# Cross attention beside its neighbours: one batch's chain in two groups, setup products in spare PSUM columns, even steps of a normalisation

## The reference

```
x = x + attention(ln1(x), ln1(x)) @ Wo1 + bo1        # 16 heads of 16, self
x = x + attention(ln2(x), ctx)   @ Wo2 + bo2         # the same, over 77 context rows ("cross")
h = ln3(x) @ Wff1 + bff1;  lin, g = split(h)
x = x + (lin * (g * sigmoid(1.702 g))) @ Wff2 + bff2 # inner width 1024
Q = x @ Wq.T + bq; K = ctx @ Wk.T + bk; V = ctx @ Wv.T + bv
x = rms_norm(softmax(Q K.T / 16) V @ Wfc.T + bfc + x) * w   # one head of 256
```

## Time and profile before

| | |
|---|---|
| median of 3 runs | 742.64 us (739.92 to 743.47) |
| the profiled execution | 749.67 us, its span 747.7 us |
| PE, DVE, ACT, POOL busy | 89%, 72%, 65%, 13% of the span |
| mean granted TensorE clock | 0.956 of full |
| chain of work that ended last, by engine | PE 64%, DVE 18%, ACT 10%, issue 5% |

### The profile page before, as it was taken

One profiled execution on the slowest core, in us unless ns is written; L12 is line 12 of the kernel. 1 busy time (PEld: TensorE's weight loads), 2 busy tenths in 40 slices (PEclk: granted clock), 3 DMA queues, 4 the chain that ended last, 5 costly groups with the idle time before them and its releaser, 6 DMA issues.

```text
span 747.7 us, 11140 instructions
## 1 busy us (share of the span) xinstructions
PE 667.3 (89%) x4072; PEld 320.0 (43%) x4072; DVE 536.1 (72%) x925; ACT 485.6 (65%) x845; POOL 93.8 (13%) x144
## 2 busy tenths in 40 slices
PE   3989799999999999999999888788798999999991
PEld 2644122222222222222224344235356878888881
DVE  6678989999999999999984538546743754343357
ACT  3543399999999999999998654447463233332374
POOL 2071800000000000000000201264101110000001
PEclk9999699999999999999999998779898999999996
DMA  9457350202020110100000020120000000000003
GB/s 301 182 169 253 95 196 1 72 1 71 1 71 2 43 30 1 29 2 29 1 2 1 31 91 23 46 70 31 3 1 1 0 1 1 1 1 1 1 0 113
DMA packets 35113, 36.87 MB, mean 49 GB/s; under 512 B 6132, under 2 KB 28276, under 8 KB 34804
## 3 DMA queue, kind: packets, MB, share of 16 engines
q1 hardware_dynamic: 33904, 35.87, 14.8%
q0 software_dynamic: 1024, 0.24, 0.3%
q10 hardware_dynamic: 132, 0.07, 0.0%
HBM read 23.09 MB, written 12.74 MB: 48 GB/s over the span
## 4 chain that ended last, share of the span: by engine, by line
PE 64%; DVE 18%; ACT 10%; issue 5%; DMA 1%; POOL 1%; SPq 0%; ACTq 0%; DVEq 0%; POOLq 0%
PE ps L934 15%; PE ps L922 10%; DVE mm L1557 7%; PE ps L718 6%; ACT probs L1317 6%; PE ps L1120 4%; PE ps L1121 4%; PE ps L1122 4%; PE ps L751 4%; PE ps L895 3%; PE ps L704 2%; PE ps L1037 2%; PE ps L726 2%; PE ps L1136 2%; DVE tok L1535 2%
## 5 line engine op out<-in xcount | busy, mean ns | idle before, releaser
L1317 ACT ACTIVATE probs<-ps,unfit 128x512 f32<-128x512 f32 x512 | 311.7, 691 | 28.6 <-PE ps L922 24.1
L1557 DVE TENSOR_REDUCE mm<-ps 128x2 f32<-128x1024 f32 x256 | 299.4, 1219 | 13.9 <-PE ps L751 9.8
L922 PE MATMUL ps<-stack 50*128 50x512 f16 x512 | 146.8, 388 | 7.2 <-ACT probs L1317 1.2
L934 PE MATMUL ps<-probs,v 128*32 128x512 f32 x1024 | 137.2, 608 | 2.7 <-ACT outT L1322 2.7
L751 PE MATMUL ps<-stack 48*128 48x512 f16 x512 | 108.5, 391 | 12.7 <-DVE mm L1557 6.6
L922 PEld LDWEIGHTS ps<-stack 50*128 50x128 f16 x512 | 36.9, 93 | 172.7 <-ACT probs L1317 164.7
L1417 ACT ACTIVATE early<-ps,cols 128x512 f32<-128x512 f32 x32 | 22.1, 690 | 91.8 <-PE ps L1122 91.8
L1813 DVE SCALAR_TENSOR_TENSOR hid<-ps,cols,early 128x512 f32<-128x512 f32 x32 | 24.0, 749 | 76.0 <-PE ps L1122 76.0
L612 POOL TENSOR_TENSOR x<-x,rows 128x512 f32<-128x512 f32 x24 | 31.9, 1343 | 164.0 <-DVE tok L1535 163.9
L1120 PE MATMUL ps<-x_hi,wff_hi 128*128 128x512 f32 x128 | 52.2, 408 | 0.0
L1372 ACT ACTIVATE probs<-ps,unfit 96x1024 f32<-96x1024 f32 x32 | 35.5, 1109 | 25.1 <-PE ps L1028 25.0
(11 more groups left out here) (168 smaller groups left out, 861.8 us busy)
## 6 DMA issues: line engine op xcount, KB each, us to landing
v_groups<-early SPq DMA_DIRECT2D x8, 512.0 KB, 3.1
stack<-q_parts SPq DMA_DIRECT2D x64, 64.0 KB, 2.0
v<-v_groups SPq DMA_DIRECT2D x8, 512.0 KB, 4.1
x<-in_x SPq DMA_DIRECT2D x4, 512.0 KB, 6.9
q_parts<-probs SPq DMA_DIRECT2D x8, 256.0 KB, 3.8
k_parts<-probs SPq DMA_DIRECT2D x8, 256.0 KB, 2.2
stack<-k_parts SPq DMA_DIRECT2D x16, 128.0 KB, 2.5
stack<-q_parts SPq DMA_DIRECT2D x64, 32.0 KB, 1.9
```

What stands on the lines that cost most here:

```text
L922: eng.matmul(ps[:, st_bank(n), :], stack[rows_of(tile, KROWS), SLOTS + slot, q, P * kc:P * kc + P], qs[rows_of(tile, KROWS), slot, half, q ...
L934: mm_ = eng.matmul(ps[32 * h:32 * h + 32, PV, :], v1[:, G % 2, kc, 32 * h:32 * h + 32], probs[:, k % 2, h, :], start=(kc == 0), stop=(kc = ...
L1317: eng.activation(probs[:, k % 2, HEADS[h], :], ps[:, st_bank(n), :], ACT.Exp, scale=unfit[:, 0:1]).then_inc(exp_done, 1)
L1557: eng.tensor_reduce(dst, ps[:, 2 * slot:2 * slot + 2, :], AX.X, ALU.max).then_inc(s_red, 1)
```

## The change

- Batch 1's chain(0,1) gets its nine pieces of the cross stage in groups 0 and 1, where they were spread over 0, 1 and 2. chain(1,0) gets all twelve of its pieces in groups 4 to 7; its last one, the turn of ln3's block 1, stood in the feed forward behind widen(0) before. `x_high(0)` and `x_low(0)` move one unit ahead.
- The first seven setup products are computed in columns 312 to 465 of banks 0 and 1, beside the 312 columns of the cross scores, just ahead of `scores_2` of tiles 10, 14, 15, 17, 19, 21 and 23, that is in (1,0), (2,0), (2,1), (2,3), (3,1), (3,3) and (4,1). DVE reads each after those scores and ahead of their maxima. The last two stand in columns 0 to 255 of these banks, after (7,0) and (7,2). Four waits of the chains and of `final_setup` go.
- `tick` goes out of `reduce_2`; each cross unit, each `add` and each `attended_2` now has tick(3).
- On SP, `load_max_2(2)` and `load_max_2(3)` stand later, behind loads of queries, and `load_q2(5)`'s first half stands behind the last store of queries.
- At the start PE turns block 0 ahead of `tops(0)`, and DVE takes `fit_scales(0)` after the statistics of block 1. POOL adds the third bias row only once eight `widen` steps are done.

```diff
-        PIECES = ((0, 1, 1, 0), (1, 1, 1, 2), (1, 1, 0, 0), (0, 0, 0, 0),
-                  (0, 0, 1, 1), (1, 1, 1, 2), (1, 1, 1, 1), (0, 0, 0, 0))
-        SETUPS = {(2, 2): 1, (2, 3): 2, (3, 1): 1, (7, 0): 1, (7, 1): 2, (7, 2): 1, (7, 3): 1}
-        SETUP_EARLY = 4
+        PIECES = ((2, 1, 1, 1), (1, 1, 1, 1), (0, 0, 0, 0), (0, 0, 0, 0),
+                  (0, 0, 1, 1), (2, 1, 2, 1), (1, 1, 0, 1), (0, 1, 0, 0))
+        SETUP_TILES = (10, 14, 15, 17, 19, 21, 23)
+        SETUPS = {(7, 0): 1, (7, 2): 1}
+        SPARE = HG * CTXE
+        def setup_col(k):
+            return SPARE if k < SETUP_1 + SETUP_2 - B else 0
...
@@ sync
             load_q2(3)
             load_max_2(1)
-            load_max_2(2)
             for u in range(half, half + NC):
                 store_parts(u)
             parts_stored(eng, half + NC)
-            for G in (4, 5):
-                eng.wait_ge(st_full, 64 * GROUPS + UNITS * (G - 3))
-                load_q2(G, (0,))
+            eng.wait_ge(st_full, 64 * GROUPS + UNITS)
+            load_q2(4, (0,))
+            load_max_2(2)
             for u in range(half + NC, len(PROJ)):
                 store_parts(u)
-            load_max_2(3)
+            eng.wait_ge(st_full, 64 * GROUPS + 2 * UNITS)
+            load_q2(5, (0,))
             parts_stored(eng, len(PROJ))
             load_q2(4, (1,))
             load_q2(5, (1,))
+            load_max_2(3)
@@ gpsimd, bias rows
+                if n == 2:
+                    eng.wait_ge(ff_full, FC)
@@ tensor
+            turn(LN1, 0)
             tops(0)
-            turn(LN1, 0)
@@ setup / final_setup
-                    bank = CHAIN + k % 2
+                    at = setup_col(k)
+                    out = ps[0:m, k % 2, at:at + n]
...
-                eng.wait_ge(rest_done, len(PROJ))
-                eng.wait_ge(su_done, SETUP_1 + SETUP_EARLY)
-                eng.wait_ge(y_added, TILES + KC)
-                turned(LN3, 0)
+                eng.wait_ge(su_done, SETUP_1 + NC)
...
+                eng.wait_ge(s2_red, KC // 2 * GROUPS)
@@ chain
-                if (n, b) == (1, 0):
-                    eng.wait_ge(su_done, SETUP_1 + SETUP_EARLY)
-                    if (ln, blk) == (LN3, 1):
-                        eng.wait_ge(su_done, SETUP_1 + SETUP_2)
@@ scores_2
                 if n >= 1:
                     eng.wait_ge(s2_red, n)
+                if n in SETUP_TILES:
+                    next(fillers)
@@ feed forward, on tensor, scalar and vector alike
+            eng.wait_ge(su_done, SETUP_1 + SETUP_2)      # tensor only
-            last_piece, after_cross = after_cross, chain(1, 1)
+            after_cross = chain(1, 1)
-                    advance(last_piece, 1)
@@ scalar, vector: x_high(0) after (7,0), was (7,1); x_low(0) after (7,1), was (7,2)
@@ vector
+                if blk == 1:
+                    fit_scales(0)
                 norm(0, blk)
-                if blk == 0:
-                    fit_scales(0)
@@ vector, chain after each add
-                    tick(4)
+                    tick(3)
@@ vector, reduce_2, attended_2, cross_unit
                 eng.wait_ge(s2_full, n + 1)
+                if n in SETUP_TILES:
+                    next(fillers)
...
-                tick(2)
...
                 attended(2 * GROUPS + 2 * G + half, MISC)
-                tick(2)
+                tick(3)
...
                     reduce_2(*divmod(ahead, UNITS))
+                tick(3)
                 advance(pieces, PIECES[G][d] // 2)
```

More of the change, by code:

```diff
@@ L301, in build @@
         AHEAD = 7
-        PIECES = ((0, 1, 1, 0), (1, 1, 1, 2), (1, 1, 0, 0), (0, 0, 0, 0),
-                  (0, 0, 1, 1), (1, 1, 1, 2), (1, 1, 1, 1), (0, 0, 0, 0))
-        SETUPS = {(2, 2): 1, (2, 3): 2, (3, 1): 1, (7, 0): 1, (7, 1): 2, (7, 2): 1, (7, 3): 1}
-        SETUP_EARLY = 4
+        PIECES = ((2, 1, 1, 1), (1, 1, 1, 1), (0, 0, 0, 0), (0, 0, 0, 0),
[3 more added lines that the diff above has]
+        SPARE = HG * CTXE
         FF_PIECES = (0, 0, 2, 2, 2, 2, 2, 2)
         assert sum(TAIL) == CHAIN_1 == AHEAD + sum(sum(PIECES[G]) for G in range(GPB))
-        assert sum(FF_PIECES) == CHAIN_2 == 1 + sum(sum(PIECES[G]) for G in range(GPB, GROUPS))
+        assert sum(FF_PIECES) == CHAIN_2 == sum(sum(PIECES[G]) for G in range(GPB, GROUPS))
         LINEAR, GATE, WIDE = 4, 5, (0, 1, 6, 7)
@@ L825, in setup @@
                 if k < SETUP_1:
-                    bank = 6 + k
+                    out = ps[0:m, 6 + k, 0:n]
                     eng.wait_ge(v_done, TILES - 1 + k)
                 else:
-                    bank = CHAIN + k % 2
+                    at = setup_col(k)
+                    out = ps[0:m, k % 2, at:at + n]
                     if k >= SETUP_1 + 2:
@@ L832, in setup @@
                 for i, (lhs, rhs) in enumerate(terms):
-                    mm_ = eng.matmul(ps[0:m, bank, 0:n], lhs, rhs, start=(i == 0), stop=(i == len(terms) - 1))
+                    mm_ = eng.matmul(out, lhs, rhs, start=(i == 0), stop=(i == len(terms) - 1))
                 mm_.then_inc(su_full, 1)
@@ L1073, in cross_unit @@
                 advance(pieces, PIECES[G][d] - PIECES[G][d] // 2)
+            fillers = final_setup()
             eng.wait_ge(mask_in, 16 * HT)
@@ L1098, in _ @@
             advance(after_self, 2)
-            fillers = final_setup()
             for G in range(GROUPS):
@@ L1398, in _ @@
                     cross_unit(G, d, after_self if G < GPB else after_cross)
-                    if (G, d) == (LAST, 1):
+                    if (G, d) == (LAST, 0):
                         x_high(0)
@@ L1420, in _ @@
                     hid_high(n - 1)
-                if n == 0:
-                    advance(last_piece, 1)
                 if n < FC:
@@ L1727, in read @@
                     eng.wait_ge(su_full, k[0])
-                    return ps[0:m, CHAIN + (k[0] - 1) % 2, 0:n]
+                    at = setup_col(k[0] - 1)
+                    return ps[0:m, (k[0] - 1) % 2, at:at + n]
                 for dst, c0 in ((kT, COL_BK), (vT, COL_BV)):
@@ L1799, in _ @@
                     advance(fillers, SETUPS.get((G, d), 0))
-                    if (G, d) == (LAST, 2):
+                    if (G, d) == (LAST, 1):
                         x_low(0)
```

## The result

Timed side by side on one chip, twenty executions each, the changed kernel took 743.30 us (median; 737.35 to 745.61) against 747.21 us (738.59 to 751.37): a ratio of 0.9947, 95% interval 0.9928 to 0.9966. It is faster by 0.5%, about 4 us, where 14 were forecast: 728.6 was predicted, and 743.3 lies outside of the range of 720 to 740. Of the 14.7 us between 728.6 and 743.3, 4.6 are not the change's: the forecast was counted from 742.64, the median of three executions of the kernel before, and its median of twenty is 747.21. The other 10.1 us are gain that did not come. Of the changed kernel's and the experiments' executions all are fast but two of `x2_spread`, which its median holds and its ratio leaves out. The profiled executions took 745.36 after and 749.67 before.

The account below looks back on a forecast made before the run. It took PE's own work plus its waits and half clock as the bound. Idle -6.3, half clock -6.5 and start -1.2 gave -14.0 us, from 742.64 to 728.6 us; range 720 to 740.

Parts of the forecast that it names:

- Idle time: From (0,0) to the end of widen(1), PE's idle time falls from 19.7 to 13.4 us: -6.3 us.
- (0,2), maximum of tile 7: `scores_2` of tile 8 waits for DVE, which has adds, statistics and scalings before tile 7's maximum: 3.1 us idle.
- (3,0), maxima's DMA: `load_max_2(3)` stands behind twelve query loads on SP, so (3,0) waits 2.4 us, between 0 and 4.
- (6,1), (6,2): DVE is full, so `scores_2` of tile 31 waits 2.5 us and `turn_max_2(7)` 1.1 us for `attended_2(5,1)`.
- behind widen(0): ln3's turns find their tokens ready, so the old stall, longest wait 2.2 us, goes; with its clock some 6 us.
- an undisturbed scaling: DVE's price for one scaling, 0.58 us, used for three scalings between the maxima of tiles 6 and 7.
- the collision of a bank's reader and writer at the setup products: Groups 2 to 4: DVE's reads between scores and maxima cost PE 0.4 us in all, bounds 0 and 3.2.
- Half clock: From (0,0) to widen(1), four half-clock stretches instead of six, each costing 3.27 us: -6.5 us.
- Groups 2 to 4 and 7 become evenly filled: Argument against half clock still coming six times once the waits shrink; no size of its own.
- the second rival: Waits shrink, but the long ones split over neighbouring units and half clock still comes six times: 735.1 us, chance 0.20.
- The third bias rows cost nothing: POOL's adds move to where POOL and DVE are busy for 2.64 and 3.83 of 13.0 us: no cost.
- The start: The turn begins where `tops` did, and 1.01 us of `tops` leave the first projection's way: -1.2 us, between 0.8 and 1.6.

Follow-up runs that it names:

- x2_spread: Changed kernel with batch 1's chain spread over groups 0 to 2 again and SP's old order there; 743.36 us, 0.9953 of the kernel before.
- x4: Changed kernel with POOL's Wff1 splits held back in batches behind DVE's splitting of the maxima; 741.06 us, 0.9933 of the kernel before.
- x7: Changed kernel with POOL's Wff1 splits spaced out and third bias adds one widen step later, no added products; 736.86 us, 0.9864 of before.
- x9: Changed kernel with Wff1 splits spaced out, bias adds one step later and nine useless dense products in (2,1) to (4,1); 730.64 us, 0.9783 of before.
- x1: Changed kernel with one useless dense f32 product behind each of nine units, (2,1) to (4,1); 739.86 us, 0.991 of the kernel before.
- x8: Changed kernel with nine useless dense products and third bias adds one widen step later; 733.93 us, 0.9835 of the kernel before.
- x11: As x9, with group 0's five chain pieces as 1, 1, 2, 1 instead of 2, 1, 1, 1; 734.29 us, 0.9841 of the kernel before.
- x10: As x9, with two useless dense products in each of the nine units instead of one; 728.77 us, 0.978 of the kernel before.
- x5: Changed kernel with POOL's third bias adds held back until nine widen steps are done, not eight; 738.43 us, 0.9879 of the kernel before.
- x12: Changed kernel without the wait ahead of POOL's third bias adds; 740.44 us, 0.9878 of the kernel before.
- x6: Kernel before with only the start changed: turn ahead of `tops`, `fit_scales` ahead of the last scalings; 748.27 us, 0.9999 of before.
- x3: Changed kernel with groups 4 to 7's old pieces, chain(1,0)'s last piece behind widen(0), `x_high` and `x_low` in old places; 745.00 us, 0.9962 of before.

## Why the prediction was wrong, step by step

**Idle time: right, a little low.** 13.4 us were forecast, 11.8 remain. By places:

| place | forecast | trace |
|---|---|---|
| (0,2), maximum of tile 7 | 3.1 | 2.15 |
| (1,1), turn of block 3 | 2.0 | 0.69 + 0.75 |
| (2,2), `attended_2` | not named | 0.34 + 1.74, and 1.21 in (3,2) |
| (3,0), maxima's DMA | 2.4 | none; 1.4 in x4 |
| (4,0), maxima's DMA | 0.9 | none |
| (6,1), (6,2) | 2.5, 1.1 | 1.29, 0.93 |
| behind widen(0) | none | none |
| all others | 1.4 | about 2.6 |

The sum came out by errors that cancel: DVE's lists were costed too long, and a wait in (2,2) was overlooked, which then covered (3,0). One price was misread: 0.58 us for an undisturbed scaling. The four scalings of a group take 1.38 us where POOL adds nothing (8.88 us, kernel before), 0.35 each, and 2.3 us where its bias adds fall on them, which is where the 0.58 came from. So the three in (0,0) were 1.03 us and not 1.74, and the collision that the third bias rows then suffered stood in the trace of before already. For the collision of a bank's reader and writer at the setup products I had taken 0.4 us; no wait there stands out.

**Half clock: the step that failed.** "Half-clock stretches: I expect one behind each of the four longer waits [...] instead of six: -2 x 3.27 = -6.5." The number was near (three), the length was not. All six stretches of before lasted 6.8 us, and I took that as a constant. In five of the six a projection, a turn or an output product stood within the stretch; in the sixth, at 500.6, one setup product did. The change gathers these in groups 0 and 1 and leaves thin products for groups 2 to 4 (48 to 50 rows deep, 78 columns, or 32-column tiles), with the setup products between them; behind one wait of 1.74 us there then were 30.7 us at half clock instead of 6.8. Forecast -6.5, measured 0. That added dense products shorten it is shown by x7 and x9, which part in nine of them alone, and by x1, where the wait stayed and the length fell to 6.8. Over all traces with the chain in two groups, the long stretch is 17.1 to 30.7 us in the six without added products and 6.8 us (x1, x8, x11) or none (x9, x10) in the five with them. What is argued, and not shown, is that the missing projections are the reason in the changed kernel: x2, which puts them back in group 2, has no half clock there, but 6.8 and 13.7 us in groups 3 and 4. Nor did any run add thin products for the same time, so it may be the added work on PE and not its shape. "Groups 2 to 4 and 7 become evenly filled" stood in the prediction as an argument against the second rival, and it was the wrong way round: filled in busy time they were, and the clock did not come back.

That rival, "the clock does not pay" (735.1 us, chance 0.20), comes nearest: the time at half clock was that of before. Its mechanism, six stretches again, was not the real one (three, one of them very long), and it lacks the bias adds too. Taken as gains, it is 7.5 us, 2.5 without the 5 us of the bias adds, and 3.9 were measured.

**"The third bias rows cost nothing": wrong.** It was argued from how little DVE and POOL had to do from 556 to 569 us, but the adds begin only when Wff1's last chunk is done, at 593.80, by the last scalings. One step later, or not held back, the kernel is 0.7% faster (x5, x12), so this cost about 5 us by the ratios; the trace of the changed kernel accounts for some 4 of them, 2.4 of waits and half of the 3.4 us at half clock. The Trainium skill's page "SBUF — State Buffer", section "Who interferes with whom", says that VectorE's scalings in a two-port mode and its instructions with two SBUF inputs exclude GpSimd for a whole instruction, and that the one which comes second blocks. By it each scaling, if it runs in such a mode, waits for one add of 1.3 us, and the trace agrees: 5.10 / 4 = 1.28 us. Which mode the scalings ran in no row shows.

**POOL's split beside the chain: not costed.** It lies earlier than before, and its instructions of 1.26 us stretch `split_max` (two SBUF inputs in L1570, 1.18 us for 0.19). This made most of the wait of 1.74 us ahead of the long stretch. It is not what the stretch needs: in x7, with the split spaced out, 30.7 us at half clock begin behind a wait of 0.75 us. Spacing it out alone gave no sure gain (x4, and x7 against x5: 0.9864 and 0.9879), since the clock stayed low for 17.1 and 30.7 us; beside dense products x9 is 3.3 us below x8, with intervals that just overlap. So its worth is likely, and not shown.

**The start: right in itself, worth nothing that the runs can tell.** The 1.0 us came, and in the changed kernel's trace 0.4 was lost again by (0,0), where a half-clock stretch stands that before did not have. Timed alone (x6) the start gave 0.9999.

**The accounts.** Forecast -14.0 us: idle -6.3, clock -6.5, start -1.2. In the traces: 0.6 ahead at (0,0), idle in the stretch -8.0, busy time +0.5, together 8.1 ahead at widen(1), and 3.9 given back behind it (2.4 us of waits for scalings, the stretch at 598.9, and DVE's late products behind them). That leaves 4.2.

The long stretch differs between executions. Kernels that are alike there have 30.7 us (changed, x3, x12) and 20.5 (x5), or 17.1 (x4) and 30.7 (x7), so its length in one profile is no measure; the comparisons above rest on the timed executions. The changed kernel's own show what the clock is worth: fifteen of the twenty have a mean granted clock of 0.949 to 0.953 and take 742.15 to 745.61 us, the other five 0.958 to 0.963 and 737.35 to 739.84. Open stays what exactly brings the clock back (at 500.6 in the kernel before, thin work with one setup product sufficed, and groups 2 to 4 of the changed kernel hold such products too), whether the shape of the added products matters or only their time, and whether useful work can take the place of the dummy products: setup products and projections are all there is, and spreading the projections (x2) brought their DMA wait back.

The best versions beat both kernels: x10 and x9 at 0.978 of before, 17 us faster and 15.4, with wasted products; without any, x7 at 0.986, x5 and x12 at 0.988.

## What to carry to other kernels

Do not cost the half clock behind a wait of PE as a constant: in this kernel it lasted 6.8 us with dense products behind the wait and up to 30.7 with thin ones. Try leaving some dense products in each thin stage, or adding useless ones where the clock stays low (here nine of 0.53 us gave back 6.2), and time it. A busy share of 90% does not show that PE is well fed; read the clock beside it, over every stage that the change leaves poorer in dense work. When a run of GpSimd instructions is moved, look up what VectorE does at the new time, and put it where no scaling or two-input instruction that PE waits for falls on it.

## What was not expected of the hardware

- PE stayed at half clock (0.50) for 30.7 us while busy for 28.95 of them, with thin products; with nine dense f32 products among them it was at full clock throughout groups 2 to 4 (x9), or at half for 6.8 us (x1, x8, x11).
- Useless work made a kernel faster: 736.86 to 730.64 us with nine products; with eighteen, 728.77, it is no slower.
- A 128x32 VectorE instruction of 0.19 us took 1.18 beside one GpSimd instruction of 1.26, and four scalings took 5.10 instead of 1.38.
- At nearly the same wait of 1.3 to 1.5 us for the queries' DMA half clock began in twelve traces, for 3.4 or 6.8 us, and in two it did not, in the kernel before and in x10.
